# Decay exponentials moved to the turn before, sixteen units in the delta rule's loop body, and the feed-forward's element-wise work dealt out anew

## The reference, cut to what matters

```python
x = x + delta_rule_attention(layernorm(x))      # x: 8 batches x 512 rows x 256
x = x + ffn(layernorm(x))
x = x + masked_attention(layernorm(x))
x = x + ffn(layernorm(x))

# the delta rule, for each of 8 batches and 8 heads (64 units), state 128x128:
for t in rows:                                   # q, k, v: causal conv of 4 taps, then silu
    state = state * exp(g_t)                     # g = -exp(A_log) * softplus(x @ Wa + dt_bias)
    for j in (0, 1):
        u = (v_t[j] - k_t[j] @ state) * beta_t[j]
        state = state + outer(k_t[j], u)
    o_t = q_t @ state
out = (rmsnorm(o) * norm_w * silu(x @ Wg)) @ Wo

def ffn(x): return relu(relu(x @ W1.T + b1) @ W2.T + b2) @ W3.T + b3
```

## Time and profile before

| | |
|---|---|
| median of 3 runs | 5268.34 us (5260.47 to 5271.86) |
| profiled execution: time, span | 5256.53 us, 5254.7 us |
| stages, from the windows of the trace | tables 0 to 175, delta rule to 3130, f to 3465, attention to 5037, h to the end |
| busy, share of span | PE 87%, DVE 54%, ACT 39%, POOL 27% |
| PE busy in the delta rule | 2606 of 2955 us |

### The profile page before, as it was taken

How to read it: one execution, slowest core, us unless ns; L and a number is a source line. 1 busy time by engine, 2 the same in 40 slices (tenths; PEclk the granted TensorE clock), 3 DMA queues, 4 the chain that set the end, 5 groups by cost and what they waited for, 6 DMA issues and landing times. The chain is left out here.

```text
span 5254.7 us, 87865 instructions
## 1 busy us (share of the span) xinstructions
PE 4563.9 (87%) x27638; PEld 3716.7 (71%) x27638; DVE 2863.7 (54%) x7411; ACT 2072.3 (39%) x5463; POOL 1425.4 (27%) x2882
## 2 busy tenths in 40 slices
PE   3588888988898888888888868978999999999979
PEld 3477777777777777777777757865666666666668
DVE  5555555555555555555555533425555555555545
ACT  2244444444444444444444412214444444444422
POOL 4233333333333333333333315620000000000024
PEclk9999999999999999999999979979999999999989
DMA  7332333222223332322333222221111111111011
GB/s 275 95 91 82 93 93 93 84 88 80 88 84 92 93 92 85 92 88 84 93 93 93 84 77 85 72 68 41 42 44 44 40 31 44 40 44 40 22 53 33
DMA packets 568788, 401.09 MB, mean 76 GB/s; under 512 B 261488, under 2 KB 513392, under 8 KB 566896
## 3 DMA queue, kind: packets, MB, share of 16 engines
q1 hardware_dynamic: 568304, 395.08, 24.4%
HBM read 296.75 MB, written 98.14 MB: 75 GB/s over the span
## 5 line engine op out<-in xcount | busy, mean ns | idle before, releaser
L886 DVE SCALAR_TENSOR_TENSOR g_conv<-g_r,g_taps,g_conv 128x511 f32<-128x511 f32 (+2 forms) x960 | 713.7, 743 | 136.6 <-ACT g_conv L785 119.8
L789 ACT ACTIVATE g_us<-g_chn 128x128 f32<-128x128 f32 x528 | 146.2, 277 | 952.6 <-PE g_chn L612 951.8
L590 PE MATMUL g_lev<-g_nu,g_T 128*128 128x128 f32 (+1 forms) x3120 | 437.3, 280 | 20.1 <-DVE g_nu L898 20.1
L559 PE MATMUL g_r<-g_x_hi,g_w_hi 128*128 128x512 f32 x768 | 356.0, 464 | 101.3 <-issue 68.2
L2195 POOL TENSOR_TENSOR a_bias<-a_kb,a_start 128x128 f32<-128x128 f32 (+2 forms) x96 | 56.6, 618 | 1381.8 <-DVE a_low L2064 941.6
L917 DVE SCALAR_TENSOR_TENSOR g_S<-g_S,g_ctab,g_chn 128x128 f32<-128x128 f32 x396 | 137.6, 347 | 526.6 <-PE g_chn L622 526.6
L583 PE MATMUL g_lev<-g_U,g_L 128*128 128x128 f32 x2340 | 346.5, 285 | 84.9 <-DVE g_L L925 43.2
L590 PEld LDWEIGHTS g_lev<-g_nu,g_T 128*128 128x128 f32 (+1 forms) x3120 | 372.9, 177 | 59.3 <-DVE g_nu L898 32.3
L1922 ACT ACTIVATE a_pr<-a_pr,a_low 128x128 f32<-128x128 f32 (+3 forms) x512 | 286.9, 560 | 314.4 <-DVE a_low L2064 310.5
L1712 PE MATMUL a_sc<-a_kT,a_qT 128*128 128x128 f32 (+3 forms) x1024 | 341.1, 460 | 60.9 <-DVE a_low L2064 56.9
L1061 POOL TENSOR_TENSOR g_prod<-g_small 64x14 f32<-64x14 f32 (+6 forms) x896 | 227.1, 254 | 587.1 <-DMA g_small<-lower_d 521.9
(11 more groups left out here) (347 smaller groups left out, 11386.9 us busy)
## 6 DMA issues: line engine op xcount, KB each, us to landing
g_w_hi<-ws_d SPq DMA_DIRECT2D x65, 768.0 KB, 5.4
g_w_lo<-ws_d SPq DMA_DIRECT2D x65, 768.0 KB, 6.5
lower_d<-g_L SPq DMA_DIRECT2D x64, 512.0 KB, 3.2
g_T<-low_d SPq DMA_DIRECT2D x64, 512.0 KB, 4.1
g_U<-upp_d SPq DMA_DIRECT2D x64, 512.0 KB, 5.3
a_w<-w_groups SPq DMA_DIRECT2D x32, 640.0 KB, 4.6
oT_d<-g_oT SPq DMA_DIRECT2D x67, 256.0 KB, 5.3
f_oT<-oT_d SPq DMA_DIRECT2D x8, 2048.0 KB, 9.0
```

What stands on the lines that cost most here:

```text
L559: mm = M.matmul(BANK[n][:], a[:, k, n, :], c[:, k, :], start=(i == 0), stop=(i == len(terms) - 1))
L590: mm = M.matmul(lev[hf][0:rows, c, :].rearrange("p (j n) -> p j n", j=2), T[0:rows, hf * HC + c, 0:rows], nu[0:rows, hf * HC + c, :].unsqu ...
L886: ins = V.scalar_tensor_tensor(out=y[:, k:L], in0=x[:, 0:L - k], scalar=tap, in1=y[:, k:L], op0=ALU.mult, op1=ALU.add)
```

## The change

1. **Exponentials earlier.** The three spreads and exponentials of unit u+1 are done in turn u, in its second half: `spread_end` after `lev_nu` 0,1, `spread_read` ahead of `chain_u` 6, `spread_start` behind it; on ACT `decay_end` after the silu of V1 (ahead of `copy_T` 0,0 and `copy_u` 6), `decay_read` and `decay_start` ahead of `copy_u` 7. `dmt` and `gam` get two buffers, the PSUM banks of the spreads change, unit 0's are done ahead of the loop, and the transposes of V wait for the last exponential. ACT ends each turn with a silu of one element, which loads silu's table there.
2. **Sixteen turns in the loop body**, four trips; the rows of x are loaded once in eight turns.
3. **`tab_d` partition first**: the store of it writes 10,240 contiguous bytes per partition.
4. POOL does the large product of `dm` ahead of two small ones.
5. **Feed-forward**: ACT rectifies and rounds all four blocks, DVE does all low parts (`low`, `heads`), POOL only `keep`; `columns` of DVE moves behind three of the second layer's low parts. The stores count on a semaphore for each parity.

```diff
 def units(eng, turn):
-    with eng.Fori(0, B) as b:
-        with eng.Fori(0, H // QN) as hp:
-            for q in range(QN):
-                turn(...)
+    with eng.Fori(0, B // 2) as i:
+        for j in (0, 1):
+            b = i * 2 + j
+            for hp in range(H // QN):
+                for q in range(QN):
+                    turn(...)
...
 # PE, turn
     project(u, par, K0)
-    pe.wait_ge(s["d_gm"], u + 1)
-    pe.wait_ge(s["d_bv"], 2 * u + 2)
-    M.matmul(dm_b[:], rep[:, 1, :], gsum[:, 1], start=True, stop=True).then_inc(s["d_dm"], 1)
-    M.matmul(dmt_b[:], rep[:, 2, :], gsum[:, 0], start=True, stop=True).then_inc(s["d_dm"], 1)
 chain_u(u, par, 0)
 ...
 chain_s(u, q, 0, made)
-    M.matmul(gam_b[:], rep[:, 0, :], gsum[:, 0], start=True, stop=True).then_inc(s["d_dm"], 1)
-    pe.wait_ge(s["d_exp"], 3 * u + 1)
+    pe.wait_ge(s["d_bv"], 2 * u + 1)
     project(u, par, V0, (0,))
 ...
 lev_nu(u, o, 0, 1, own)
+    pe.wait_ge(s["d_gate"], u + 3)
+    spread_end(u + 1)
 chain_u(u, par, 5)
 ...
 lev_T(u, o, 0, 1)
+    pe.wait_ge(s["d_conv"], 5 * u + 6)
+    spread_read(u + 1)
 chain_u(u, par, 6)
+    spread_start(u + 1)          # waits for the first exponential of u + 1
 ...
     transposes of V
+    pe.wait_ge(s["d_exp"], 3 * u + 6)
 # ACT, turn
-    exponentials of unit u around copy_u 0
 copy_u(u, 5)
     silu(u, q, V1)
+    act.wait_ge(s["d_L"], 2 * u + 4)
+    decay_end(u + 1)
+    copy_T(u, 0, 0)
 copy_u(u, 6)
-    copy_T(u, 0, 0)
     copy_T(u, 0, 1)
+    decay_read(u + 1, 1 - par)
+    act.wait_ge(s["d_qg"], u + 1)
+    decay_start(u + 1, 1 - par)
 copy_u(u, 7)
 ...
     squares of q
+    A(tiny[:], tiny[:], ACT.Silu)
 # SP
-    if q == QN - 1:
+    if hp * QN + q == H - 1:
         sp.wait_ge(s["d_proj"], NB * u + NB + 1)
-        rows(b + hp)
+        rows(b + 1)
 # tables
-io["tab_d"] = nc.dram_tensor("tab_d", (B * H + 1, P, 5 * NC), F32).ap()
+io["tab_d"] = nc.dram_tensor("tab_d", (P, B * H + 1, 5 * NC), F32).ap()
 # feed-forward, DVE
 def turn(b, par, first, more):
-    for n in (0, 2):
-        high(b, n, h1_hi, ...); relu(b, n + 1, b1, ...)
+    for n in range(N1):
+        low(b, n, h1_hi, h1_lo, "h1_hi", "h1_lo")
     if not first:
         result(b - 1, 1 - par)
     if more:
         norm(b + 1, 1 - par)
-    high(b, 0, ...); relu(b, 1, ...); high(b, 2, ...)
-    if more:
-        columns(b + 1)
-    relu(b, 3, ...)
+    if split:
+        heads(b + 2, (0, 1, 2, 3))
+    second(0)                       # second = low of layer two
+    if split:
+        heads(b + 2, (4, 5))
+    second(1)
+    if split:
+        heads(b + 2, (6, 7))
+    second(2)
+    if more:
+        columns(b + 1)
+    second(3)
```

More of the change, by code:

```diff
@@ L1403, in columns, with low, heads @@
                     V.tensor_tensor(x_lo[:, k, :], xps[k][:], x_hi[:, k, :], ALU.subtract).then_inc(s["x_lo"], 1)
[L1405 to L1414 removed]
+            def low(b, n, hi, lo, have, sem):
+                dve.wait_ge(s[have], 4 * b + n + 1)
+                V.tensor_tensor(lo[:, n, :], hs[:, n, :], hi[:, n, :], ALU.subtract).then_inc(s[sem], 1)
+            def heads(b, hs_):
+                for h in hs_:
+                    dve.wait_ge(s["o_hi"], H * b + h + 1)
+                    V.tensor_tensor(o_lo[:, h, :], oT[:, h, :], o_hi[:, h, :], ALU.subtract).then_inc(s["o_lo"], 1)
             def result(b, par):
@@ L1423, in turn @@
             def turn(b, par, first, more):
-                for n in (0, 2):
-                    high(b, n, h1_hi, "h1a", "h1vh")
-                    relu(b, n + 1, b1, "l1", ("h2_lo", -4), first, "h1v")
+                second = lambda n: low(b, n, h2_hi, h2_lo, "h2_hi", "h2_lo")
+                split = delta_out and more == 2
+                for n in range(N1):
+                    low(b, n, h1_hi, h1_lo, "h1_hi", "h1_lo")
                 if not first:
@@ L1491, in turn, with split, _, keep @@
                 second(2)
+                if more:
+                    columns(b + 1)
                 second(3)
+            def split(i):
+                pair, raw, _ = weights[i]
+                dve.wait_ge(s["w_hi"], i + 1)
+                V.tensor_tensor(flat(pair[1]), raw[:, 0:pair[0].shape[1] * pair[0].shape[2]], flat(pair[0]), ALU.subtract).then_inc(s["w_lo"], 1)
+            dve.wait_ge(s["eps"], 1)
+            split(0)
             if delta_out:
                 heads(0, range(H))
+                split(1)
+            norm(0, 0)
+            columns(0)
+            for i in range(2 if delta_out else 1, len(weights)):
+                split(i)
+            if delta_out:
+                heads(1, range(H))
+            turns(dve, turn)
+            result(B - 1, 1)
+        @block.gpsimd
+        def _(pool):
+            G = nc.gpsimd
+            G.memset(eps[:], LN_EPS).then_inc(s["eps"], 1)
+            G.memset(start[:], 0.0).then_inc(s["y"], 1)
+            def keep(b, par, first):
+                pool.wait_ge(s["xin"], b + 1)
+                if not first:
+                    pool.wait_ge(s[f"out{par}"], 8 * b - 8 * par)
+                G.tensor_tensor(xb[par][:], x[par][:], b3[:].unsqueeze(1).to_broadcast([P, TT, D]), ALU.add).then_inc(s["xb"], 1)
+            def turn(b, par, first, more):
+                if more:
+                    keep(b + 1, 1 - par, first)
             pool.wait_ge(s["bias"], 48)
             keep(0, 0, True)
-            if delta_out:
-                heads(1, range(H))
             turns(pool, turn)
-FFN_SEMS = ["x0", "x1", "oT", "id", "bias", "wo_in", "w1_in", "w2_in", "w3_in", "w_hi", "w_lo", "o_hi", "o_lo", "y", "out", "wo", "xn", "tr",
-            "x_hi", "x_lo", "l1", "l2", "l3", "h1a", "h1v", "h1ah", "h1vh", "h1_lo", "h2a", "h2v", "h2ah", "h2vh", "h2_lo",
+FFN_SEMS = ["x0", "x1", "oT", "id", "bias", "wo_in", "w1_in", "w2_in", "w3_in", "w_hi", "w_lo", "o_hi", "o_lo", "y", "out0", "out1", "wo", "xn", "tr",
+            "x_hi", "x_lo", "l1", "l2", "l3", "h1", "h1_hi", "h1_lo", "h2", "h2_hi", "h2_lo",
             "mv", "std", "xin", "xb", "eps", "dve"]
```

146 lines of the change are left out of this document (59 added, 87 removed).

## The result

The changed kernel takes 5100.4 us (median of 4 runs, 5096.3 to 5101.3) against 5270.1 us (4 runs, 5260.5 to 5273.7): ratio 0.9679, 95% interval 0.9662 to 0.9696. The forecast was 5130 us in a range from 5110 to 5175. The profiled execution takes 5096.3 us (span 5094.5), against 5256.5 of before: 160 us less.

A forecast was written before the change was run, and what follows sets the result against it. PE (87% busy) bounds, idling in short waits behind ACT or DVE. 30 + 45 + 11 - 11 + 38.5 + 4 - 1.5 + 19 + 3 = 138 us off 5256.5 leaves 5118.5; plus 11.8 to the median, 5130, range 5110 to 5175.

The forecast's parts named there:

- early exponentials (30+45+11-11-1.5): Delta rule: spreads moved 30, stall ahead of L622 45, K1's silu wait 11, middle loss -11, unit 0's spreads -1.5 us.
- feed-forward f and h: Feed-forward stages: subtractions moved from POOL to DVE shorten PE's waits, 19 us in f and 3 in h.
- It shows in 42 of 56 turns, three of four, so 48 of 64: 45 us: Turn's front: PE's stall ahead of L622, behind ACT's table load and exponential, costs 0.93 us a time and leaves.
- A loop end so costs 3.2 us: Delta rule's loop ends: 2.1 us idle on average, the rest overlap and slower trips; 12 fewer ends bring 38.5 us.
- some trips that run slower after it: Behind loop ends: with overlap, the part of the 3.2 us an end costs beyond its 2.1 us average idle.
- the front of the turn: From `project(K0)` to L622: two spreads moved away bring 0.47 us a turn, the stall ahead of L622 0.93.
- The loss in the middle: At `lev_nu` 1,0: ACT's T copy comes later behind table load and exponential, losing 0.17 us a turn, 11 us.
- The wait for K1's silu: Ahead of K1's transposes: remains almost whole, since DVE's taps end last; shrinks about 0.17 us a turn, 11 us.
- ACT's order in the middle: Rival, 15%: in the turn's middle, T's copy or `us` comes 0.7 us later than placed, 45 us: 5175.
- drain at a table switch: ACT's table switches: skill's rule adds 1.38 us, losing 88 us; rival of a second 1.28 us, 4%: 5212.
- Longer bodies: Slower rival, 4%: instruction supply gives a sixteen-turn body gaps like a loop's end inside; at every turn, 5326.
- More than forecast: Rival, 6%: `lower` comes earlier by POOL's new order and f loses all its waits: 5110.

The follow-up runs named there:

- second profile of before: The kernel before, unchanged, executed once more for its profile: 5270.5 us, against 5256.5 us in its first profile.
- idle time put back: The changed kernel with four turns in the body and a useless 2048-column copy on ACT ahead of the turn's first copy `us`: 5231.0 us.

## Why the prediction fell short: parts priced alone, gained together

The parts by the medians, against the forecast's sum:

```
part                                       forecast   measured alone
early exponentials (30+45+11-11-1.5)           73        75
sixteen turns in the body                      38.5      40
feed-forward f and h                           22        32
tab_d's store                                   4        (4: the rest of the 170)
both large parts together, beyond the two       0        20
sum                                           138       170
```

The 20 are 59.6 less 40.1, what the long body gives in the changed kernel and in the kernel before. They are a difference of four medians, each of runs that spread over 5 to 16 us. `tab_d` had no run of its own; the trace has its store at 4.5 us instead of 10.0, and the first projection 3.2 us earlier (187.5 instead of 190.7).

**The step that failed** is the count in "It shows in 42 of 56 turns, three of four, so 48 of 64: 45 us". The stall is missing in the fourth turn because the loop's end stands there and hides it. For the kernel as it was, that is the right number. But the same change takes 12 of those ends away. Without them the stall would be in 60 turns (the run with the long loop alone shows it in 51 from 300 to 2700 us, against 40), and the early exponentials remove it there too: 12 times 0.93 us, 11 of the 20. With it fails a second term, "A loop end so costs 3.2 us", which was held to be the same in either kernel. Seen from the loop, an end costs 3.3 us against a turn with a stall (3.0 and the 0.33 ahead of it, in the second profile of before) and 4.7 against one without.

The other 9 us are in the main the clock, as far as the record can tell. The slow matmuls stand behind 11 of 15 ends in the second profile of before, and behind all 15 in both runs with early exponentials, a short loop and no idle time put back, with 121 and 126 of them against 90. Each timed execution also has its granted clock, and one less that share, times the span, is an estimate, an upper one, of what the lower clock cost it. On average it is 149 us in the 27 timed executions of the kernel before, 126 with the long body alone, 147 in the changed kernel with the short loop and 116 in the changed kernel. The long body so gives back 23 us of clock where the exponentials stand in front and 31 where they are early. Taken from the two runs with the new feed-forward and the exponentials in front (137 us with the short loop, 112 with the long body), the 23 become 25. That leaves 6 to 8 us at most, from clocks recorded to 0.001, which is 5 us. With the 11 it makes 17 to 19 of the 20, and by the turns it is 17 (4.7 less 3.3, twelve times). The last 1 to 3 us have no cause here. I had the clock in the 3.2 us as "some trips that run slower after it" and took it as constant. That the clock falls at each end once the exponentials are early is what both profiles show; why, is open. Neither the gap's length nor the density of the turns ahead of it sorts the ends in these traces, and moving the one copy of `us` in the kernel before was enough for 15 of 15. One thing does go with it where the exponentials stand in front: every second end closes the outer loop too, and in the three profiles whose delta rule is that of the kernel before, the clock fell behind 20 of these 21 ends and behind 8 of the 24 others. Whether that is the kind of end or the moment at which it comes is open.

**The first profile was a lucky one.** The prediction put the median 11.8 us above its sum as a constant. The second profile shows the difference to lie in the turns with a loop end (46.26 and 47.13 us on average, 15 of them, 13 us), where it has the more slow matmuls, and a change to the loop removes these with the ends. It is part of why 160 us between two profiles are 170 between medians: the changed kernel's profiled execution lies 4.0 us under its median, that of before 13.6. It also made the loop's term right by luck. The prediction took four turns without an end to last 175.9 us, but with the stall back in the turn whose end goes they are 177.0 (two of 44.17, one of 44.49, one more of 44.17). By that profile an end then costs 2.4 us instead of 3.2 (46.26 less 44.17, and 0.32 ahead of it), and twelve of them 29 us. The 40 measured are those of slower executions, like the second profile, where an end costs 3.3.

**Right**, point by point: the front of the turn, 0.47 and 0.93 us (1.40 measured at the state's product). The loss in the middle, 0.17 us forecast and 0.13 measured; whether by T's copy, as described, or by the third spread is not shown. The later `us` of chunk 6 had room. The wait for K1's silu stays; it shrank by 0.2 us, and K1's transposes come 0.31 us earlier beyond the 1.40, where I had 0.17. With the middle's loss taken off, a turn without an end became 1.58 us shorter, 0.18 more than the 1.40 I summed. The small silu covers its load; without it the kernel takes 9 us more. `tab_d` and the loads of x cost nothing elsewhere. f's first product waits 5.8 us less (forecast 6), batch 1's 5.5 less (4.9).

**The feed-forward** was mis-sized by 10 us. In steady turns `layer_one` waits 1.74 us (forecast 2.0), but a turn became 1.8 us shorter (38.21 to 36.38, from one `layer_one` to the next), not 1.3. From f's first product to the attention's first scores it is 370 to 377 us in the profiles with the new distribution and 390 to 396 in those without, about 21 us less, where the forecast had 13 behind f's start. h gained 5 us, not 3.

**Rivals.** None came true. ACT's order in the middle costs no more than the main case had for it. The Trainium skill's drain at a table switch (ScalarE: Activation LUTs, What ACT_TABLE_LOAD costs) does not show at L822 either, and without the small silu the whole switch cost 0.2 us. Longer bodies show no gaps inside. "More than forecast" had the right side and half of a reason. f and h gave 10 us more, though f did not lose all its waits. `lower` gave nothing of its own, since PE's wait for it is 33.3 us in the changed kernel and 32.7 with the long loop alone (300 to 2700 us). The product of the two main parts is missing in it, and for that the 6% given to it and the lower end at 5110 were too tight: the range was built from single mechanisms, each with its own bound (48 us for the loop), and never from two terms that depend on each other.

## What to carry to other kernels

Where a change removes two delays that lie beside each other, work the sum out on the schedule that is left, not on that of before: a stall that is missing in some turns is hidden by something there, and if that leaves as well, the stall's price counts in all turns. Before a profiled execution is taken as the base, look at how its rare events (here the half-clock stretches behind loop ends) compare with the spread of the timed runs, and treat the difference as part of what the change touches. What stands ahead of a table load or an exponential on ACT is still worth an order of its own: moving one copy of T, with a bank of its own for the third spread, gave 14 us more.

## What the runs showed of the hardware

A loop's back edge costs PE 1.3 to 2.8 us of idle time, and no more with a longer body: 2.1 to 2.2 us on average in the seven profiles with four-turn bodies, 1.3 to 2.0 in those with sixteen. The Trainium skill (Runtime: NRT & Kernel Launch, Instruction fetch mechanics) says that a taken branch outside the fetched pages has to wait for a fetch; a cost that doesn't grow with the body agrees with that.

Behind such a gap TensorE ran at 1.2 GHz for 4 to 12 of the projection's matmuls and was back at 2.4 within about 7 us, in most ends but not all: in the kernel before behind 7 ends in one execution and behind 11 in another. It was there behind a gap of 1.76 us (910.06 above) and did not come at all behind one of 2.25 us (at 1815.44 in the same run, granted clock 1.00 from 1815 to 1820). That moves an unchanged kernel by some 14 us: this is what its two profiles differ by, and of its 27 timed executions the fastest (5258.5 us) has a granted clock of 0.974 and the slowest (5275.5) one of 0.970.
